# Expert routing scores taken from the centred tokens in pairs, and half-wise waits ahead of the expert products

## The reference, cut to what matters

```python
x2 = (h - mean(h)) / sqrt(var(h) + 1e-5)           # over the 64 features
gate_scores = x2 @ Wg + bg                          # (tokens, 8)
_, idx = top_k(gate_scores, 2)
mask = one_hot(idx, 8).sum(-2)
hid = gelu(einsum('td,edh->teh', x2, W1) + b1)      # exact gelu
y = einsum('teh,ehd->ted', hid, W2) + b2
h = h + einsum('ted,te->td', y, mask)
```

## Time and profile before

| | |
|---|---|
| Time, median of 3 runs | 207.59 us (206.76, 207.59, 209.97) |
| Profiled execution, its own time | 207.45 us |
| Its span in the trace | 205.7 us |
| Mean granted TensorE clock | 0.807 of full speed |
| PE busy | 142.7 us, 69% of the span |
| PE weight loads | 87.8 us, 43% |
| DVE busy | 130.6 us, 63% |
| ACT busy | 73.1 us, 36% |
| POOL busy | 35.5 us, 17% |
| Chain that ended last | DVE 39%, PE 36%, issue 10%, ACT 5%, DMA 5% |

### The profile page before, as it was taken

How to read it: one execution, slowest core, us unless ns; L and a number is a source line. 1 busy time by engine, 2 the same in 40 slices (tenths; PEclk the granted TensorE clock), 3 DMA queues, 4 the chain that set the end, 5 groups by cost and what they waited for, 6 DMA issues and landing times.

```text
span 205.7 us, 2099 instructions
## 1 busy us (share of the span) xinstructions
PE 142.7 (69%) x690; PEld 87.8 (43%) x690; DVE 130.6 (63%) x342; ACT 73.1 (36%) x122; POOL 35.5 (17%) x52
## 2 busy tenths in 40 slices
PE   0889839208829969079959700176999998869991
PEld 0552623207226733075848600165665635435440
DVE  2649995679990589899886999937441572603011
ACT  2010510352060481186681203042643364354541
POOL 2031510128200264234320203120000000000000
PEclk9999966955965885856985965555799999999999
DMA  5999800000000000000000000000000000002011
GB/s 141 289 393 365 356 18 29 0 0 0 0 0 0 0 0 0 0 3 2 2 0 0 5 0 0 0 0 0 0 5 0 0 0 3 0 0 51 0 26 26
DMA packets 7042, 8.80 MB, mean 43 GB/s; under 512 B 2388, under 2 KB 4436, under 8 KB 7032
## 3 DMA queue, kind: packets, MB, share of 16 engines
q1 hardware_dynamic: 7032, 8.68, 12.8%
HBM read 8.15 MB, written 0.52 MB: 42 GB/s over the span
## 4 chain that ended last, share of the span: by engine, by line
DVE 39%; PE 36%; issue 10%; ACT 5%; DMA 5%; POOL 2%; SPq 1%; DVEq 0%; POOLq 0%; ACTq 0%
PE bank L899 7%; DMA dist_sb<-in_dist 5%; PE bank L883 4%; PE bank L884 3%; PE bank L638 3%; PE bank L859 3%; DVE dist_sb L990 2%; DVE q_sc L1171 2%; PE bank L777 2%; DVE proj L1061 2%; DVE invpos L995 2%; DVE rs_v L958 1%; DVE mask_in L1228 1%; DVE proj L1062 1%; PE bank L909 1%
## 5 line engine op out<-in xcount | busy, mean ns | idle before, releaser
L584 ACT ACTIVATE hid<-bank 128x512 f32<-128x512 f32 x32 | 17.7, 597 | 22.6 <-PE bank L884 22.6
L899 PE MATMUL bank<-hid,ffn_sb 128*64 128x512 f32 x64 | 16.8, 615 | 0.0
L883 PE MATMUL bank<-xp,w1hi 128*128 128x512 f32 x32 | 14.6, 457 | 0.7 <-ACT xp L568 0.7
L1274 DVE TENSOR_TENSOR h<-bank,h 128x256 f32<-128x256 f32 x4 | 1.7, 422 | 21.0 <-PE bank L909 21.0
L853 PE MATMUL bank<-early_sb,xhl 128*128 128x128 f32 x16 | 3.1, 352 | 14.7 <-DVE xhl L1245 14.7
L884 PE MATMUL bank<-xp,w1lo 96*128 96x512 f32 x32 | 12.7, 397 | 0.0
L1189 DVE TENSOR_TENSOR dist_sb<-bank,early_sb 128x256 f32<-128x256 f32 x16 | 6.1, 420 | 10.0 <-PE bank L782 8.8
L990 DVE TENSOR_TENSOR dist_sb<-dist_sb,mask_in 128x1024 f32<-128x1024 f32 x8 | 9.5, 1231 | 4.3 <-POOL mask_in L326 4.2
L654 PE MATMUL bank<-early_sb,vk 128*128 128x128 f32 x8 | 2.2, 435 | 13.7 <-DVE vk L1040 13.7
L638 PE MATMUL bank<-dist_sb,neigh 128*64 128x512 f32 x32 | 11.4, 787 | 0.0
L696 PE MATMUL bank<-late_sb,proj 128*128 128x8 f32 x16 | 3.8, 364 | 11.1 <-ACT proj L466 11.1
(11 more groups left out here) (246 smaller groups left out, 365.0 us busy)
## 6 DMA issues: line engine op xcount, KB each, us to landing
dist_sb<-in_dist SPq DMA_DIRECT2D x4, 1024.0 KB, 11.0
mask_in<-in_mask SPq DMA_DIRECT2D x4, 256.0 KB, 10.1
ffn_sb<-in_ffn SPq DMA_DIRECT2D x1, 813.0 KB, 10.9
fold_sb<-in_folded SPq DMA_DIRECT2D x1, 772.0 KB, 12.3
late_sb<-in_late SPq DMA_DIRECT2D x1, 728.5 KB, 11.5
out<-h SPq DMA_DIRECT2D x8, 64.0 KB, 1.7
early_sb<-in_early SPq DMA_DIRECT2D x1, 391.0 KB, 3.1
mask_in<-in_mrows SPq DMA_DIRECT2D x1, 128.0 KB, 2.3
```

Source lines behind the costliest of these rows:

```text
L584: nc.scalar.activation(hid[:, at % HB], bank[hid_bank[at % 3]][:, :], ACT.Gelu).then_inc(S["hid_set"], 1)
L883: nc.tensor.matmul(o, w1hi[:, e * HID:(e + 1) * HID], xp1[g][:, toks], start=True, stop=False)
L899: mm = nc.tensor.matmul(bank[2][j * D:(j + 1) * D, :], K["e_w2"][:, (e + j) * D:(e + j + 1) * D], hid[:, (at + j) % HB], start=False, stop ...
```

## The change

The scores are formed from x2 as it is after centring, before the factor st_r is known. PE transposes the centred x2 by pairs in step #1 (4 transposes), ACT copies them to a new tile x2_t behind its square, and PE forms the scores in step #2 with 4 matmuls against a block-diagonal Wg of 16 columns. DVE multiplies the scores by st_r out of PSUM and adds bg in one more operation. DVE now waits for the transposes (x2t_mm) before it overwrites x2 with the normalised tokens. Step #3 on PE keeps only the 8 transposes of xhl. The flag transposes wait for the copy of xp1 half by half. The products wait for the first half of xp2 ahead of n = 0, and for the second ahead of n = 8 (in group 0 ahead of n = 1). The DMAs are the same but for 8 more columns in the expert weights' tile.

```diff
-FFN = [("wg", P, E), ("bg", P, E), ...
+FFN = [("wg_bd", P, 2 * E), ("bg", P, E), ...
+        x2_t = sb("x2_t", [P, L])
@@ ACT, experts, step #1
                 nc.scalar.activation(sq[:, :, 0:D], v8(x2[:]), ACT.Square, scale=D ** -0.5).then_inc(S["x2_sq"], 1)
+                act.wait_ge(S["x2t_mm"], g + 1)
+                nc.scalar.copy(x2_t[:, :], bank[x_bank[g]][:, :]).then_inc(S["x2t_set"], 1)
@@ PE, experts
-                yield
-                yield
-                pe.wait_ge(S["xhl_set"], g + 1)
                 i = x_bank[g]
+                pe.wait_ge(S["x2_centred"], g + 1)
                 if g == 0:
                     pe.wait_ge(S["gate_read"], NG)
                     pe.wait_ge(S["st_set"], NG)
+                for c in range(NC):
+                    mm = nc.tensor.transpose(bank[i][:, c * P:(c + 1) * P], pair(x2, c), ident)
+                mm.then_inc(S["x2t_mm"], 1)
+                yield
+                pe.wait_ge(S["x2t_set"], g + 1)
+                if g == 0:
+                    pe.wait_ge(S["center_set"], 2 * NG)
+                for c in range(NC):
+                    mm = nc.tensor.matmul(bank[i + 3][:, c * 2 * E:(c + 1) * 2 * E], x2_t[:, c * P:(c + 1) * P], K["wg_bd"],
+                                          start=True, stop=True)
+                mm.then_inc(S["score_mm"], 1)
+                yield
+                pe.wait_ge(S["xhl_set"], g + 1)
                 f32 = xhl[:].bitcast(F32)
                 for n in range(2):
                     for t in range(4):
                         mm = nc.tensor.transpose(bank[i + n][:, t * P:(t + 1) * P], f32[:, 4 * n + t, 0:2 * D], ident)
                     mm.then_inc(S["xp1_mm"], 1)
-                pe.wait_ge(S["xp1_set"], 2 * g + 2)
-                if g == 0:
-                    pe.wait_ge(S["center_set"], 2 * NG)
-                for t in range(8):
-                    mm = nc.tensor.matmul(bank[i + 3][:, t * E:(t + 1) * E], xp1[g][:, t * P:(t + 1) * P].bitcast(F32), K["wg"],
-                                          start=True, stop=True)
-                mm.then_inc(S["score_mm"], 1)
                 yield
                 yield
                 pe.wait_ge(S["mask_set"], g + 1)
                 for n in range(2):
+                    pe.wait_ge(S["xp1_set"], 2 * g + n + 1)
...
-                pe.wait_ge(S["xp2_set"], 2 * g + 2)
...
                 def hidden(n):
                     k, e = n // E, n % E
+                    if n == 0:
+                        pe.wait_ge(S["xp2_set"], 2 * g + 1)
+                    if n == E or (n == 1 and g == 0):
+                        pe.wait_ge(S["xp2_set"], 2 * g + 2)
@@ DVE, experts, steps #2 and #4
                 rsqrt(st_r[:, :], 8)
+                dve.wait_ge(S["x2t_mm"], g + 1)
                 link(nc.vector.tensor_tensor(v8(x2[:]), v8(x2[:]), bc(st_r[:, :], D), ALU.mult))
...
                 nc.vector.tensor_tensor(score[:], bank[x_bank[g] + 3][:, 0:64].rearrange("p (t e) -> p t e", e=E),
-                                        rows_bc(K["bg"], 8), ALU.add).then_inc(S["score_read"], 1)
+                                        bc(st_r[:, :], E), ALU.mult).then_inc(S["score_read"], 1)
                 dve.wait_ge(S["score_read"], g + 1)
+                link(nc.vector.tensor_tensor(score[:], score[:], rows_bc(K["bg"], 8), ALU.add))
@@ the packing of the weights
-        "wg": np.tile(arr(L0_ffn_Wg), (2, 1)), ...
+        "wg_bd": bd(L0_ffn_Wg), ...
```

More of the change, by code:

```diff
@@ L75 @@
         ("hop2w_bd", P, 2 * H), ("hop_b2w", P, H)]
-FFN = [("wg", P, E), ("bg", P, E), ("e_w1", P, E * HID), ("e_w2", P, E * D), ("e_b2", P, D),
+FFN = [("wg_bd", P, 2 * E), ("bg", P, E), ("e_w1", P, E * HID), ("e_w2", P, E * D), ("e_b2", P, D),
        ("tie", P, E), ("sel_hi", P, 1), ("sel_lo", P, 1)]
@@ L249, in tower @@
             cct_set attn_mm h3_set hx_set
-            x2_centred x2_sq xhl_set xp1_mm xp1_set score_mm score_read mask_set xp2_mm xp2_set w1_hi w1_lo
+            x2_centred x2_sq x2t_mm x2t_set xhl_set xp1_mm xp1_set score_mm score_read mask_set xp2_mm xp2_set w1_hi w1_lo
             hid_mm hid_set b2_hi b2_lo y_mm y_copied yt_mm y_set""".split()
@@ L1352 @@
     ffn = pack(FFN, {
-        "wg": np.tile(arr(L0_ffn_Wg), (2, 1)), "bg": row(L0_ffn_bg), "e_w1": np.tile(e_w1, (2, 1)),
+        "wg_bd": bd(L0_ffn_Wg), "bg": row(L0_ffn_bg), "e_w1": np.tile(e_w1, (2, 1)),
         "e_w2": arr(L0_ffn_W2).transpose(1, 0, 2).reshape(HID, E * D), "e_b2": e_b2,
```

## The result

The changed kernel takes 202.01 us (median of four executions, 201.91 to 202.40) against 207.18 before (206.01 to 209.97): ratio 0.974, 95% interval 0.969 to 0.980. The profiled execution took 201.98 us, span 200.3. Forecast was 202.2.

The account below looks back on a forecast made before the run. Before 147 us the chain through DVE was taken as the bound, then PE. From 207.45 us, minus 3.98, 1.05 and 0.8 gives 201.6, with the clock 202.1, with the median's offset 202.2 us; range 200.8 to 204.8.

Parts of the forecast that it names:

- the stand in X1: PE, among group 0's last products, waits about 1.35 us for DVE to centre group 1's x2 before transposing it.
- Part 1, group 0: Group 0's routing: DVE loses its 4.24 us wait for scores, pays 0.26 for one added operation; net gain 3.98 us.
- Part 2, group 1: Group 1's routing on PE: flag transposes 1.05 us earlier, plus 0.8 us from waiting for single halves of the copies.
- closed holes: PE's idle in group 1's routing, at copies of the first transposes and at the flags, 0.73 us each, goes.
- half-wise wait: Group 1's first product needs only the first copy, so ACT's GELU follows the second copy directly; gain 0.8 us.
- The clock: PE's granted clock around group 0's first products: a loss of 0.5 us, between a gain of 0.9 and a loss of 1.8.
- upper bound: Clock rise stays at 147.0 us while products start at 143.2: some 3.6 us at half speed, a loss of 1.8.
- one of the signs: Prediction is wrong if the lower-clock stretch ends later relative to the first expert product; no size given.
- Rival 1: The clock rises late at group 0's products, after fewer PE passes ahead: 203.4 us; chance 0.17.
- Rival 2: Group 1 gives nothing, PE's new stand and ACT's copy between GELUs are not paid back: 203.5 us; chance 0.13.
- Rival 3: Group 0 gives nothing, another input such as cosine product or sine holds the query sums: 205.6 us; chance 0.05.
- Rival 4: Slower: the clock falls in PE's new stand for group 1's centring; 6.5 us low costs 3.3; chance 0.03.

Follow-up runs that it names:

- e1: the kernel before with only the half-wise waits on the copies of xp1 and xp2; median 207.49 us, ratio 0.996.
- e4: the changed kernel measured again on another chip, no edit; median 203.42 us, ratio 0.978 to the kernel before.
- e5: the changed kernel with a POOL cosine product of group 0 cut to a sixteenth, not the one beside the bias operation; 201.31 us, ratio 0.970.
- e2: the kernel before with the new score path in group 0 alone and half-wise waits only for the flag transposes; median 205.92 us, ratio 0.989.
- e7: the changed kernel with group 1's x2 transposes and copy one position later and its scores behind product 12 of group 0; 201.34 us, ratio 0.964.
- e10: the changed kernel with the POOL product beside the added bias operation (group 1's last cosine product) cut to a sixteenth; 204.16 us, ratio 0.980.
- e11: the changed kernel without the bias of the scores and its added operation; 205.28 us, ratio 0.986.
- e6: the changed kernel with unread PE transposes added, 20 behind group 0's scores and 24 behind the key transposes; median 202.30 us, ratio 0.973.
- e9: the changed kernel with both the later group 1 transposes and scores of e7 and the added PE transposes of e8; median 199.39 us, ratio 0.956.
- e8: the changed kernel with unread PE transposes added, 20 behind group 0's scores and 42 behind the key transposes; median 201.24 us, ratio 0.967.
- e3: the kernel before with the new score path in group 1 alone and half-wise waits only for the flag transposes; median 206.16 us, ratio 0.989.

## Why the prediction was right, and where its terms were off

**The mechanism was right.** The idle of 4.24 us before the score operation is gone, its place on DVE's queue is taken over by nothing else, and the query sums moved up with it. The scores end at 127.1 (forecast 127.2), the stand in X1 is 1.36 us (1.35), the flag transposes of group 1 gain 1.11 us (1.05). One reading was loose without harm to the sum: the transposes of xhl end at 134.75 us, 0.7 before DVE begins to stand, so the 4.24 us hold the copies and the scores alone.

**Part 1, group 0: 3.98 forecast, 3.47 measured at the flags.** The term that was off is the added operation: 0.26 us from a row in which POOL was idle, 0.86 in its new place (135.24 to the start of the next one at 136.10). Moving the top-2 earlier moved it beside POOL's product, which I had looked at only as an input that comes in time. I could have read the hold in the trace of the kernel before. Its inverse root has an operation with two inputs in SBUF beside POOL's first product, and it ends as the product ends (129.61 and 129.59 us):

```profile
128.54 1.05 POOL L393 TENSOR_TENSOR q_sc<-q_sc,mag 128x512 f32<-128x512 f32 x1 [2.36 <-ACT q_sc L515]
128.69 0.92 DVE L947 TENSOR_TENSOR rs_u<-rs_a,rs_v 128x8 f32<-128x8 f32 x1
```

The same operation takes 0.17 us at every other place in that trace.

**Part 2, group 1: 1.85 forecast, 1.43 measured.** The closed holes were right. The half-wise wait was put at 0.8 us, on the reasoning that the GELU would follow the second copy without idle; it was 0.33 (e1). The first product was taken to be done by then, but it starts 0.25 us behind the first copy and takes 0.7 us itself. Its own length was missing from the sum. So 0.83 us of idle before the GELU became 0.51, not nothing.

**The clock.** I took a loss of 0.5 with bounds of -0.9 and +1.8. The first profile has 0.16 us gained in stage A beyond the flags; e4 has 2.92 lost (of 3.48 at the flags 0.56 remained at the end of A). So the upper bound was too small. It ended the lower level where the kernel before had ended it, at 147 us, and counted 3.6 us of products; e4 stays down for 7.0 us of them. (The gain in the lower bound took its 1.94 and 1.08 us from the rows of the flag transposes; the query transposes took 1.70.)

The first profile is the best case of all those with the new routing in group 0 and nothing added on PE. Rises are read from windows of 0.5 us:

| profile | first product starts | level rises | products at the lower level | stage A |
|---|---|---|---|---|
| changed, first | 143.19 | 142.9 | 0 | 33.42 |
| e5 | 143.21 | 144.1 | 0.9 | 34.05 |
| e2 | 144.11 | 147.2 | 3.1 | 34.74 |
| e7 | 144.04 | 147.2 | 3.2 | 34.83 |
| e10 | 142.18 | 145.5 | 3.3 | 34.29 |
| e11 | 143.01 | 149.9 | 6.9 | 35.95 |
| e4 | 141.37 | 148.35 | 7.0 | 36.49 |

In e10 and e11 the flags come 0.60 and 0.51 us sooner than in the others, which lowers their stage A by as much. In all but the first the level rises behind the first product, which is one of the signs by which the prediction would call itself wrong; its sum has 0.5 us for it where these stages lose 0.6 to 3.1 against the first. The Trainium skill, "TensorE: Matmul & The Clock Gate", section "What's actually happening", has activity release the throttled level; that taking PE's work away can delay the release, which I drew from it and gave little weight, is nearer to these six than my sum. In e6 and e9, with 20 transposes more behind the scores, the level rose 7.2 and 7.3 us after the centring starts, against 13.2 or more in every profile without them; but in e8, with the same 20, it took 13.6.

That the forecast total was met within 0.2 us is therefore partly luck: two terms were 0.9 us too good together, and in the first profile that was made up by the clock, with a gain of 0.16 where a loss of 0.5 was forecast, and by the 0.39 us ahead of the centring. On another chip the median was 203.42. Both lie in the range.

**The rivals.** Rival 1, the late clock, got a chance of 0.17 and is the case in all six later profiles of the table, though at its full size of 1.8 us or more over the first only in e4 and e11. Rival 2 (group 1 gives nothing) falls to e3. Rival 3 (the top-2 held nothing up) falls to PE's query transposes, which wait for the query sums and start 19.13 us after the centring starts, against 22.59 before (141.83 and the earlier trace rows). Rival 4, the clock falling at the stand, did not occur in any of the eight profiles with the stand: all have 1.00 from 160 to 193 us. The one fall late in the products is in e2, where group 1 has the old routing and no stand.

**Left open.** Why two executions of the same code differ in the clock's place was not settled, only what it costs in the stages that were profiled. How often each case comes was not counted either. And the mean granted clock does not order the totals: e9 took 196.41 us at 0.842 and 201.09 at 0.846, e8 199.67 at 0.841 and 202.29 at 0.843. Only one execution of each was profiled, so what makes up those differences is not shown.

## What to carry to other kernels

A small product that waits for a scale factor can be formed from the unscaled data when the scale is per row: here that took 4.24 us of idle from the engine that bounds, for one more operation on it. When an operation is moved, look at what runs beside it in the new place, not only at what it waits for; with VectorE and GpSimd both at work, two inputs in SBUF are the sign. And where a PE-bound stretch follows a quiet one, its clock level can be worth as much as the edit (3.07 us in stage A here): try PE at work up to the first real product, as in e8, and read gains of part edits from landmarks of the timeline, since the executions of one kernel spread over up to 5 us.

## What the runs showed that I had not expected

- One and the same kernel's stage A took 33.42 and 36.49 us. The flags came at the same time in it, and behind them the granted clock differed.
- The level rose to 1.00 in the changed kernel while PE stood still (136.1 to 139.4 us, no PE instruction), after 16 transposes from 132.4 to 136.1; in the kernel before, 3.58 us of score matmuls from 136.07 to 139.65 were followed by no rise, and the level came up only at 147 us.
- 62 transposes that nothing reads did not make the kernel slower and made stage A shorter: 32.88 us, and 32.86 in e9, against 33.42 and 36.49. The total was 201.24 us, against 202.01 and 203.42 on other chips.
- An operation of 128x8 elements took 0.92 us in place of 0.17 in the kernel before, beside a product on POOL.
